# A three-layer transformer block on one core: the rotation of the queries by a second projection, replaced by a VectorE product across the two halves of the partitions; the pipeline written out; the first loads in another order

## The reference

```
x = x + 0.5 * ffn(layernorm(x))        # stream f1
x = x + attention(layernorm(x))        # stream at
x = x + 0.5 * ffn(layernorm(x))        # stream f2

ffn:  probs = sigmoid(x @ router.T);  weights of the best two of 8 experts, normalised
      y = sum over experts e of weight[e] * relu(x @ w1[e])**2 @ w2[e]
attention: q, k, v = x @ W_qkv;  q, k = rope(q), rope(k)      # 16 heads of 8
      rope(q) = q*cos + rotate_half(q)*sin
      qf = elu(q/sqrt(8)) + 1;  kf = elu(k) + 1
      out = (qf @ (kf.T @ v)) / max(qf @ sum(kf), 1e-6);  out @ W_out
```

## Time and profile before

| what | value |
|---|---|
| median of 3 runs | 827.89 us (826.98 to 828.34) |
| the profiled execution | 823.68 us, its span 821.5 us |
| mean granted TensorE clock | 0.978 |
| busy share | PE 90%, POOL 83%, ACT 73%, DVE 72% |

### The profile page before, as it was taken

The page is one execution under the profiler, slowest core; times in us unless marked ns, Lnnn a source line. Parts: engine busy times, 40 slices in busy tenths (PEclk is TensorE's granted clock), DMA queues, the critical chain, the costliest instruction groups (busy, mean ns, idle before and its releaser), DMA issues.

```text
span 821.5 us, 14132 instructions
## 1 busy us (share of the span) xinstructions
PE 737.2 (90%) x3648; PEld 598.1 (73%) x3648; DVE 588.3 (72%) x1820; ACT 599.2 (73%) x1219; POOL 685.2 (83%) x668
## 2 busy tenths in 40 slices
PE   1679888889999999999899998999999989789887
PEld 1457666767887888878687886878887868667665
DVE  3454678777879798887679687787888577676553
ACT  3567686667787879787687877788877765766765
POOL 4587868869999999999799997999989877675876
PEclk9998999989999999999999999999999999989999
DMA  5443023023233331312333230223333303303330
GB/s 173 167 156 115 28 104 104 1 103 104 104 105 116 104 118 67 107 56 106 108 103 116 103 116 21 107 92 103 117 104 117 116 2 104 94 24 117 116 116 26
DMA packets 31009, 79.25 MB, mean 96 GB/s; under 512 B 3296, under 2 KB 14304, under 8 KB 30944
## 3 DMA queue, kind: packets, MB, share of 16 engines
q1 hardware_dynamic: 28672, 76.03, 27.2%
q10 hardware_dynamic: 2272, 2.51, 0.9%
HBM read 73.81 MB, written 4.72 MB: 96 GB/s over the span
## 4 chain that ended last, share of the span: by engine, by line
PE 45%; POOL 15%; DVE 13%; issue 12%; ACT 10%; DMA 4%; DVEq 0%; POOLq 0%; ACTq 0%; SPq 0%
POOL h_lo L888 9%; PE bank L512 6%; PE bank L530 5%; PE bank L514 5%; PE bank L513 5%; PE bank L531 5%; PE bank L532 5%; DVE hid L1060 4%; ACT h_hi L763 3%; PE bank L563 3%; DMA g_all_f<-rows_f 3%; PE bank L493 2%; ACT hid L752 2%; PE bank L614 2%; ACT xn_f L709 2%
## 5 line engine op out<-in xcount | busy, mean ns | idle before, releaser
L888 POOL TENSOR_TENSOR h_lo<-hid,h_hi 128x512 fp32r<-128x512 f32 x384 | 493.8, 1309 | 97.0 <-ACT h_hi L763 96.3
L1060 DVE SCALAR_TENSOR_TENSOR hid<-bank,g_all_f 128x512 f32<-128x512 f32 x384 | 262.2, 684 | 155.2 <-PE bank L514 121.9
L752 ACT ACTIVATE hid<-hid 128x512 f32<-128x512 f32 x384 | 228.8, 621 | 47.9 <-DVE hid L1060 47.3
L763 ACT ACTIVATE h_hi<-hid 128x512 fp32r<-128x512 f32 x384 | 225.5, 620 | 4.3
L512 PE MATMUL bank<-x_hi_f,w_hi 128*128 128x512 f32 x384 | 165.7, 431 | 21.5 <-DVE hid L1060 20.3
L530 PE MATMUL bank<-h_hi,w_hi 128*128 128x512 f32 x384 | 156.9, 409 | 17.8 <-ACT yT L774 10.6
L531 PE MATMUL bank<-h_lo,w_hi 128*128 128x512 f32 x384 | 153.9, 401 | 0.0
L514 PE MATMUL bank<-x_hi_f,w_lo 128*128 128x512 f32 x384 | 153.7, 400 | 0.0
L532 PE MATMUL bank<-h_hi,w_lo 128*128 128x512 f32 x384 | 153.4, 399 | 0.0
L513 PE MATMUL bank<-x_lo_f,w_hi 128*128 128x512 f32 x384 | 152.9, 398 | 0.0
L512 PEld LDWEIGHTS bank<-x_hi_f,w_hi 128*128 128x128 f32 x384 | 73.9, 192 | 48.0 <-DVE hid L1060 29.7
(11 more groups left out here) (106 smaller groups left out, 1055.2 us busy)
## 6 DMA issues: line engine op xcount, KB each, us to landing
g_all_f<-rows_f SPq DMA_DIRECT2D x128, 512.0 KB, 5.2
x_sb<-in_x SPq DMA_DIRECT2D x16, 256.0 KB, 3.8
out_x<-x_sb SPq DMA_DIRECT2D x16, 256.0 KB, 6.8
g_all_f<-in_w ACTq DMA_DIRECT2D x2, 768.0 KB, 7.2
con<-in_const ACTq DMA_DIRECT2D x1, 652.0 KB, 7.4
rows_f<-g_row_f SPq DMA_DIRECT2D x32, 16.0 KB, 1.4
g_all_f<-in_wqkv ACTq DMA_DIRECT2D x1, 192.0 KB, 9.2
wout_sb<-in_wout ACTq DMA_DIRECT2D x1, 64.0 KB, 6.9
```

The lines of the kernel that those rows point to most:

```text
L752: fn(h, h, ACT.Square).then_inc(s_sq[s], 1)
L763: fn(h_hi[:, c, :], hid[:, c % STAGE, :], ACT.Copy).then_inc(s_hhi[s], 1)
L888: gp.tensor_tensor(h_lo[:, c, :], hid[:, c % STAGE, :], h_hi[:, c, :].bitcast(F32), ALU.subtract).then_inc(s_hlo[s], 1)
L1060: v.scalar_tensor_tensor(hid[:, c % STAGE, :], hp[c % 2][:], 0.0, g_all[s][:, EXPERT[c], :], ALU.max, ALU.mult).then_inc(s_z[s], 1)
```

## The change

It has three parts.

1. One projection of the queries. `q_rotated` is gone. DVE takes the product with sin across the halves: two instructions of 64 partitions, each of which reads PSUM and the constant in one half and writes `qb` in the other (`sin_q` is stored with its halves exchanged). The product with cos is then taken in place in a0. The second half of `kv` goes to bank a1.
2. `pipeline` has no loop: all iterations are straight code, t = -3 to 21.
3. At the start, SP's queue takes nearly all loads, in the order x group 0, w1, x group 1, most of the constants, w2, x group 2, wqkv, wout, x group 3. ACT's has the first 136 columns of the constants (identity and expert numbers) and the router. `w1_hi` comes after the first `norm` on ACT; `w2_hi` and `w2_lo` come at the end of iteration -2.

```diff
 def pipeline(eng, iteration):
 
-    for t0, trips in runs():
-        if trips == 1:
-            for u in range(2):
-                iteration(t0 + u, (t0 + u) % 2)
-        else:
-            with eng.Fori(0, trips) as i:
-                for u in range(2):
-                    iteration(Step(i, 2, t0 + u, trips), (t0 + u) % 2)
-
+    for t in range(T_FIRST, T_LAST + 1):
+        iteration(t, t % 2)
...
-            for n in range(4):
-                load(n, n % 2)
+            first_part = WHERE["expert"][1]
+            load(0, 0)
+            sp.dma_start(w1_raw, w1).then_inc(s_w1, 16)
+            load(1, 1)
+            sp.dma_start(con[:, first_part:], const[:, first_part:]).then_inc(s_con, 16)
+            sp.dma_start(w2_raw.rearrange("p (c d) -> p c d", c=NC), w2.rearrange("(c p) d -> p c d", p=P)) \
+                .then_inc(s_w2, 16)
+            load(2, 0)
+            sp.dma_start(wqkv_raw, wqkv).then_inc(s_wqkv, 16)
+            sp.dma_start(wout_sb[:], wout).then_inc(s_wout, 16)
+            load(3, 1)
...
-            def q_rotated(n):
-                if not live(n):
-                    return
-                if due(n):
-                    pe.wait_ge(A["atT"], value(n))
-                q_proj(n, 1, a1[:]).then_inc(A["qr"], 1)
...
-            act.wait_ge(s_w1, 16)
-            fn(w1_hi[:], w1_raw, ACT.Copy).then_inc(s_w1hi, 1)
...
+                if first_time(True, t + 3):
+                    act.wait_ge(s_w1, 16)
+                    fn(w1_hi[:], w1_raw, ACT.Copy).then_inc(s_w1hi, 1)
+                if first_time(True, t + 2):
+                    act.wait_ge(s_w2, 16)
+                    fn(w2_hi[:], w2_raw.rearrange("p (c d) -> p c d", c=NC), ACT.Copy).then_inc(s_w2hi, 1)
...
+            def rope_q_sin(n):
+
+                if live(n):
+                    if first_time(True, n):
+                        dve.wait_ge(s_con, 16)
+                    dve.wait_ge(A["q"], value(n + 1))
+                    for here, there in ((0, P // 2), (P // 2, 0)):
+                        i = v.tensor_tensor(qb[here:here + P // 2], q_sum[there:there + P // 2],
+                                            sin_q[there:there + P // 2], ALU.mult)
+                    i.then_inc(A["qb"], 1)
+
             def rope_q_cos(n):
                 if live(n):
-                    dve.wait_ge(A["q"], value(n + 1))
-                    if due(n):
-                        dve.wait_ge(A["qf"], value(n))
-                    v.tensor_tensor(qa[:], a0[:].rearrange("p (b t) -> p b t", b=BG), cos_q, ALU.mult).then_inc(A["qa"], 1)
+                    v.tensor_tensor(q_sum, q_sum, cos_q, ALU.mult).then_inc(A["qa"], 1)
...
-                rope_q_cos(t - 1)
+                rope_q_sin(t - 1)
...
-                rope_q_sin(t - 1)
+                rope_q_cos(t - 1)
```

More of the change, by code:

```diff
@@ L168, in constant_columns @@
     cos_k, sin_k = cos[:, col_f], sin[:, col_f] * sign
+    swapped = (np.arange(D) + D // 2) % D
     scale = np.float32(HD ** -0.5)
@@ L174, in constant_columns @@
         "ident": np.eye(P),
+        "expert": np.broadcast_to(np.arange(EXP)[None, :], (P, EXP)),
         "cos_q": cos_k[tok].T * scale,
-        "sin_q": sin_k[tok].T * scale,
+        "sin_q": (sin_k[tok].T * scale)[swapped],
         "cos_k": cos_k.reshape(P, RT * D),
@@ L290, in build @@
         a0, a1, a2 = bank[5:8]
-        q_sum = a1[:].rearrange("p (b t) -> p b t", b=BG)
+        q_sum = a0[:].rearrange("p (b t) -> p b t", b=BG)
         s_load = [sem(f"s_load{u}") for u in range(2)]
-        s_w1, s_w2, s_con, s_wqkv, s_router, s_wout = (
-            sem(n) for n in ("s_w1", "s_w2", "s_con", "s_wqkv", "s_router", "s_wout"))
+        s_w1, s_w2, s_ident, s_con, s_wqkv, s_router, s_wout = (
+            sem(n) for n in ("s_w1", "s_w2", "s_ident", "s_con", "s_wqkv", "s_router", "s_wout"))
         s_store = sem("s_store")
@@ L564, in split_product @@
                 return i
-            def q_proj(n, rot, o):
-                hi, lo = x_hi["at"][0][:], x_lo["at"][0][:]
-                return split_product(o, [(wq_hi[:, rot, :], hi), (wq_hi[:, rot, :], lo), (wq_lo[:, rot, :], hi)])
             def q(n):
@@ L593, in kv @@
                 else:
-                    pe.wait_ge(A["qa"], value(n + 1))
+                    if due(n):
+                        pe.wait_ge(A["atT"], value(n))
                 for r in range(RT):
@@ L646, in out_proj @@
                 i.then_inc(A["y"], 1)
-            pe.wait_ge(s_con, 16)
+            pe.wait_ge(s_ident, 16)
             def iteration(t, par):
@@ L807, in iteration @@
                 squares(t - 1, 7)
-                if first_time(True, t + 2):
-                    act.wait_ge(s_w2, 16)
-                    fn(w2_hi[:], w2_raw.rearrange("p (c d) -> p c d", c=NC), ACT.Copy).then_inc(s_w2hi, 1)
                 norm("at", t - 1)
@@ L894, in iteration @@
                 remainders(t - 1, 23)
-                if first_time(True, t + 2):
-                    pool.wait_ge(s_w2hi, 1)
-                    gp.tensor_tensor(w2_lo[:], w2_raw.rearrange("p (c d) -> p c d", c=NC),
-                                     w2_hi[:].bitcast(F32), ALU.subtract).then_inc(s_w2lo, 1)
                 remainders(t, 0, 1)
@@ L914, in iteration @@
                 remainders(t, 20)
+                if first_time(True, t + 2):
+                    pool.wait_ge(s_w2hi, 1)
+                    gp.tensor_tensor(w2_lo[:], w2_raw.rearrange("p (c d) -> p c d", c=NC),
+                                     w2_hi[:].bitcast(F32), ALU.subtract).then_inc(s_w2lo, 1)
             pipeline(pool, iteration)
```

55 lines of the change are left out of this document (14 added, 41 removed).

## The result

The changed kernel takes 803.96 us (median of 4 runs, 802.61 to 804.86) against 828.12 us for the kernel before on the same chip: 0.9711 of its time, 95% interval 0.9682 to 0.974. That is 24 us faster, where I had predicted 16.5 and a time of 811.4. The profiled execution took 804.86 us, the longest of its four.

The account below looks back on a forecast made before the run. PE was taken as nearly the bound (44.22 of 44.75 us per full iteration), POOL next. Loop 8.15 + rotation 4.3 + start 4.1 = 16.5 us, giving 811.4 us against the median; range 804.5 to 819.5.

Parts of the forecast that it names:

- The loop: Loop returns at t=8 to 9 and 10 to 11: writing the loop out saves 8.15 us, at least 6.86.
- The stands: DVE stood 3.34 and 3.52 us ahead of kf at the loop's returns; none of 3 us should remain.
- The rotation: Dropping the second projection frees PE 0.70 us per group, DVE pays 0.84: 4.3 us in ten full iterations, at most 7.0.
- 1.27 - 0.84 = 0.43: Gain in us per full iteration: DVE's slack behind the sine product less the added time of the two half products.
- the tail of VectorE behind the slack: DVE and ACT part of a full iteration's chain, after PE's dense part until PE resumes at 309.31: 8.1 us.
- the six thinner ones: Rotation in the filling and draining iterations, t = 1 to 3 and 14 to 16: zero together, between -2.5 and +2.
- The start: Earlier x of group 0 and reordered weight splits: 2.4 + 0.2 + 1.5 = 4.1 us, bounds 1.5 and 4.8.
- POOL's 42.59 us still fits: POOL's busy time per full iteration would still fit in the predicted iteration of about 44.3 us.
- The base: The runs' median was 4.2 us above the profiled 823.68 us, so the predicted 807.2 became 811.4.
- The rivals: DVE replaces PE, 0.17; start gives nothing, 0.10; half partitions take half time, 0.10; straight code brings stands, 0.07; slower, 0.04.
- The third: Half the partitions take half the time, so DVE pays nothing for the rotation: 21 us gained, 806.6; chance 0.10.

Follow-up runs that it names:

- b_straight: The kernel before with only the pipeline loop written out as straight code: 817.69 us, ratio 0.9882, full iteration 44.74 us.
- b_newstart: The kernel before with only the new order of loads and weight splits, loop and both projections kept: 824.88 us, ratio 0.9959.
- a_nocross: The changed kernel, but each half product reads and writes the same half of the partitions, so nothing is crossed (output wrong): 802.37 us, ratio 0.9697.
- a_oldstart: The changed kernel with the old order of first loads and weight splits, keeping straight code and one projection: 808.73 us, ratio 0.9764.
- r_oneinput: The changed kernel with POOL's root power made a product and chosen_f a reduction with one SBUF input (output wrong): 783.55 us, ratio 0.9442.

## Why the prediction was wrong

**The loop.** The stands are gone, and no full iteration is above the usual. Predicted 8.15 us; b_straight measured 9.8 (6 to 13.5). Right, at the low side: the trace that gave 8.15 was of an execution in which TensorE's clock fell behind one return (0.96) and not behind the other (1.00). In b_newstart's it fell behind both, and the loop cost 12.2.

**The rotation, the step that failed.** "PE loses 0.70 us in each of 16 groups. That is the most it can give per iteration": it gave 1.18. The price on VectorE was about right: 0.84 predicted for three losses of overlap of 0.08 each, 0.93 measured from the hid ahead (0.72 + 0.71 + 0.71 us against 0.61 + 0.60), since each loss is 0.1. a_nocross bears out the rule that I weighed (the Trainium skill, VectorE: DVE Perf Modes, Two Vector instructions with no wait between them), by which the change of halves is what costs the overlap: 0.61 us to the hid where the halves are the same, 0.71 where they change. What failed is the sum around it: 1.27 - 0.84 = 0.43 took the tail of VectorE behind the slack, 8.1 us, as fixed. It was not. It held two waits for POOL's h_lo, 0.69 and 0.18 us, inside the durations of chosen_f and ka, where no wait is listed. PE's earlier matmuls moved the order against POOL's, and these waits fell to 0 (with 0.23 more in kf). That is 0.64 us off VectorE's tail; on PE, 0.48 of it arrived. I had read the 8.1 us from the chain and asked only when it begins, not why 64 columns take 0.88 us. (It is also 7.9 us, from 301.41 to 309.31, and not 8.1.) A row that I quoted showed such a wait: nbias at 1.82 us beside w_lo. Predicted 4.3 us in the ten full iterations and zero in the six thinner ones; measured 9.8 on straight code, 10.4 of it in the full iterations and about zero in the others.

How the shift would fall was luck, and no row before could have priced it: the same PE work is worth 0 us of a full iteration with POOL's power gone, and 1.17 with it.

**The start.** Predicted 4.1, measured 4.4 by the ratios and 3.4 in b_newstart; kf at t = 2 came 3.5 us earlier. x landed at 4.38 us (0.75 + 3.63) where I had 3.9, and the root started 3.98 us earlier, but only 2.26 earlier than a_oldstart's, whose nbias was not held.

**POOL.** "POOL's 42.59 us still fits" held: its busy time is 43.05 of 43.58 us. It stands in the chain for 39% but does not bound the iteration by its work, since with 3 us less of it the iteration was longer. Only when the hold was gone too did the iteration fall below 43.57.

**The base.** The profiled execution before, 823.68 us, lay 4.2 us under the median, and I had put the median back on. That was right: 826.5 to 829.4 in the later comparisons.

**The rivals.** None of the five was it. The third gave nearly the measured time, 806.6, for a reason that is false: each half lasts as long as the whole, 0.69 us. That its number lies nearer than the forecast is chance.

What stays open: the late broadcast at the end of the profiled execution after (hid waits 5.89 us for it) is seen in some executions and not tried; and what sets how long VectorE stands at the loop's return. Why the returns cost 8 us in one execution and 12 in another is seen in the granted clock above; why it falls in one and not in the other is open too.

## What to carry to other kernels

When a short instruction takes several times what its columns ask (64 columns: 0.88 us against 0.19), look at what the neighbour engine runs at its end, before taking the stretch around it as fixed. Put a VectorE instruction that POOL's h_lo holds where VectorE waits for something anyway, or change its form, and measure the new form: the reduction with one input was free, the comparison with a value per partition was not. When such a stretch is in the cycle, expect a small shift of any engine to be worth anything from nothing to more than itself. Measure the parts on top of one another and not only alone: the projection gave 6.0 us under the loop and 9.8 without it, even if the difference is not clear of the intervals.

## What the runs showed of the hardware

- A VectorE instruction with two SBUF inputs (chosen_f, pick_f, cw_f, the sum of ka and kb, kf) that starts while POOL's h_lo runs is held by up to 1.1 us, to the end of h_lo. In the trace of the kernel before, 22 of 22 chosen_f and 20 of 20 pick_f that started with over 0.3 us of h_lo to go were. The reduction with one SBUF input never was, in 17 of 17 (r_oneinput).
- It works the other way too: POOL's h_lo took 1.57 us in the changed kernel behind the sum of ka and kb, 1.31 on the mean, and in the kernel before its nbias took 1.82 us behind w_lo, 0.20 when it started first.
- One input is no safeguard. VectorE's copy of xT from SBUF to SBUF (CAST, 128x512), 0.41 us when free, took up to 1.53 us in the changed kernel, and was held in 21 of 21 cases where it started with over 0.3 us of h_lo to go; a comparison with a value per partition (8 columns) took 0.22 us at the median and up to 1.34.
- POOL's powers don't hold VectorE for their length: in the changed kernel the sum of ka and kb started at 300.74 and ran its 0.68 us, while root_f (299.41, 1.64 us) was still running; 14 chosen_f started with 0.7 us or more of root_f to go and took 0.22.
- Two VectorE products of 64x512 last 0.69 us each, as one of 128x512 does, and start 0.71 us apart where neighbours on the same partitions are 0.60 apart.
- Less work on an engine that is almost the bound made the kernel's full iteration 1.08 us longer (43.57 to 44.65).
